# Attention mask as 64 rows of the score stacks, one stack per head, in place of mask matmuls and GpSimd selects

## What is computed

```python
x = x + 0.5 * ffn(layernorm(x))    # 8 experts, each token to its best one, hidden width 512
x = x + attn(layernorm(x))
x = x + 0.5 * ffn(layernorm(x))

def attn(x):
    xn = x * rsqrt(mean(x * x) + EPS) * norm_w
    q, k, v = heads(xn @ Wq.T + bq), heads(xn @ Wk.T + bk), heads(xn @ Wv.T + bv)   # 16 heads of 8
    scores = einsum('bhqd,bhkd->bhqk', q, k) / sqrt(8)
    scores = where(triu(ones((256, 256)), k=1), -inf, scores)
    out = einsum('bhqk,bhkd->bhqd', softmax(scores), v)
    return xn + out @ Wo.T + bo
```

## Time and profile before

| | |
|---|---|
| median of three runs | 322.96 us |
| profiled execution, its span | 319.3 us |
| PE busy | 276.5 us (87%) |
| DVE busy | 214.5 us (67%) |
| POOL busy | 178.8 us (56%) |
| ACT busy | 159.7 us (50%) |
| attention loop | about 127 to 240 us of the span |
| expert parts | about 41 to 86 and 264 to 308 us |

### The profile page before, as it was taken

The page is one execution under the profiler, slowest core; times in us unless marked ns, Lnnn a source line. Parts: engine busy times, 40 slices in busy tenths (PEclk is TensorE's granted clock), DMA queues, the critical chain, the costliest instruction groups (busy, mean ns, idle before and its releaser), DMA issues.

```text
span 319.3 us, 7990 instructions
## 1 busy us (share of the span) xinstructions
PE 276.5 (87%) x2396; PEld 224.1 (70%) x2396; DVE 214.5 (67%) x691; ACT 159.7 (50%) x389; POOL 178.8 (56%) x319
## 2 busy tenths in 40 slices
PE   8573999999995776999999999998977699999960
PEld 8463999999994363656666566665646588999960
DVE  3877048788608759987666777776787555888850
ACT  2430076666204834586666667768541107666620
POOL 5577815554525201587777787788657730554551
PEclk9855999999999998799999999999976579999996
DMA  6973141220040731662524522110001143222100
GB/s 180 403 293 119 53 95 54 65 63 31 24 126 8 199 121 53 197 180 88 156 79 134 152 72 74 57 53 6 3 19 42 42 121 86 51 67 71 34 10 0
DMA packets 34387, 29.37 MB, mean 92 GB/s; under 512 B 4108, under 2 KB 28817, under 8 KB 34352
## 3 DMA queue, kind: packets, MB, share of 16 engines
q1 hardware_dynamic: 29696, 23.52, 24.6%
q0 software_dynamic: 2496, 4.27, 4.1%
q10 hardware_dynamic: 2160, 1.14, 1.4%
HBM read 17.08 MB, written 12.55 MB: 93 GB/s over the span
## 4 chain that ended last, share of the span: by engine, by line
PE 58%; POOL 11%; DVE 10%; issue 7%; DMA 5%; ACT 4%; POOLq 1%; ACTq 0%; SPq 0%; DVEq 0%
PE bank L1279 13%; PE bank L1290 12%; PE bank L1207 5%; PE bank L1436 3%; PE bank L1408 3%; PE bank L1384 3%; POOL pT L541 2%; POOL row L454 2%; PE bank L1381 2%; PE bank L1414 2%; PE bank L1271 2%; POOL disp_d L462 2%; PE bank L1240 2%; PE bank L1466 2%; PE bank L1389 1%
## 5 line engine op out<-in xcount | busy, mean ns | idle before, releaser
L723 ACT ACTIVATE pT<-bank 128x512 f32<-128x512 f32 x96 | 56.4, 599 | 36.2 <-PE bank L1414 25.2
L1207 PE MATMUL bank<-zero 128*128 128x128 f32 x298 | 43.2, 314 | 9.4 <-DVE rowi L916 4.7
L1279 PE MATMUL bank<-xsT,ew 128*128 128x128 f32 x368 | 48.8, 276 | 0.2
L1290 PE MATMUL bank<-experts,hT 128*128 x368 | 48.9, 276 | 0.0
L1207 PEld LDWEIGHTS bank<-zero 128*128 128x128 f32 x298 | 41.6, 227 | 10.1 <-DVE rowi L916 4.7
L1038 DVE TENSOR_REDUCE mh<-bank 128x2 f32<-128x512 f32 x64 | 42.1, 682 | 8.5 <-PE bank L1384 8.2
L541 POOL TENSOR_SCALAR_AFFINE_SELECT pT<-pT 128x512 f32<-128x512 f32 x62 | 39.8, 643 | 10.2 <-ACT pT L723 9.9
L1279 PEld LDWEIGHTS bank<-xsT,ew 128*128 128x128 f32 x368 | 44.7, 192 | 0.7 <-ACT xsT L621 0.3
L1290 PEld LDWEIGHTS bank<-experts,hT 128*128 128x128 f32 x368 | 44.8, 192 | 0.5 <-issue 0.3
L627 ACT ACTIVATE hT<-bank,ew 128x128 f32<-128x128 f32 x92 | 28.8, 364 | 28.9 <-PE bank L1279 28.9
L923 DVE TENSOR_SCALAR hT<-bank,ew 128x128 f32<-128x128 f32 x92 | 28.0, 346 | 20.2 <-PE bank L1279 18.9
(11 more groups left out here) (133 smaller groups left out, 479.4 us busy)
## 6 DMA issues: line engine op xcount, KB each, us to landing
sp_d<-spl SPq DMA_DIRECT2D x32, 192.0 KB, 2.6
experts<-in_experts SPq DMA_DIRECT2D x8, 578.0 KB
qz<-sp_d SPq DMA_DIRECT2D x32, 96.0 KB
ks<-sp_d SPq DMA_DIRECT2D x32, 96.0 KB
xs_sb<-disp_d SPq DMA_DIRECT2D x46, 66.0 KB, 1.8
row<-in_x SPq DMA_DIRECT2D x4, 256.0 KB, 5.5
row<-x_d SPq DMA_DIRECT2D x4, 256.0 KB, 5.0
disp_d<-pad ACTq DMA_DIRECT2D x12, 66.0 KB, 2.3
```

The lines of the kernel that those rows point to most:

```text
L723: act.activation(pT[:, u, :], bank[2 + u % 2][:, :], ACT.Exp, scale=SCALE).then_inc(a_e, 1)
L1207: pe.matmul(bank[b][:, 0:P], zero[:, :], zero[:, :], start=True, stop=True)
L1279: mm = pe.matmul(bank[2 + 2 * (k % 2) + c // 2][:, (c % 2) * P:(c % 2 + 1) * P], ew[:, k % WRING, c * P:(c + 1) * P], xsT[:, k % 2, :], st ...
L1290: mm = pe.matmul(bank[6 + k % 2][:, 0:D], hT[:, k % 2, c, :], w2.rearrange("p a c -> p (a c)"), start=(c == 0), stop=(c == HC - 1))
```

## The change

The contraction grows to 128 rows and carries the mask itself. A stack now holds one head: rows 0 to 47 the parts, 48 to 50 the maxima (-1 on the side of `ks`), 63 to 127 the mask: one row for each of the 64 blocks of two tokens (for the last block one in each half of the sequence, so 65), whose products of powers of two give a sum of at most -2^45 where a key is later than its query, and exactly zero elsewhere. `ks` has as many stacks as `qz`, 16 each. Every unit of either product becomes four matmuls of 128 columns, one a head, with weights of its own. Blocks that need no mask use 65 rows. The identity matmuls, the selects, DVE's `last_mask`, the table `low` and the semaphore `a_pm` are gone; `pv` waits for the exponentials themselves.

The constant rows come from a new input, `tri` (128 x 512 float32, 256 KB), loaded by the sync engine ahead of the expert weights. `stack_fill` is now a broadcast copy of it: POOL fills one `qz`, ACT the other `qz` and both `ks`, between the exponentials of the first routing and behind the pad rows. Since the queries' product now passes the rows of the maxima, `stack_load` for sequences from 2 on first writes zeros over them with a DMA of its own, and the waits of `scores_q` count 80 instead of 64 for these.

```diff
-JROWS = BLK * HD
-SROWS = 2 * JROWS
+SROWS = BLK * HD
 MROW = SROWS
 KROWS = MROW + 3
+TROW = 65
+UP, DOWN, NEXT, FAR = 40, -41, 5, 86
...
+def stack_rows():
+    c = np.zeros((P, 2, T), np.float32)
+    c[MROW:KROWS, 1, :] = -1
+    t = np.arange(T)
+    for row, block, half in ([(TROW - 2, P // 2 - 1, 0), (TROW - 1, P // 2 - 1, 1)]
+                             + [(TROW + r, r, None) for r in range(P // 2 - 1)]):
+        here = np.ones(T, bool) if half is None else t // P == half
+        n = t % P
+        last = block == P // 2 - 1
+        c[row, 0, here & (n == 2 * block)] = 2.0 ** UP
+        if not last:
+            c[row, 0, here & (n == 2 * block + 1)] = 2.0 ** DOWN
+        c[row, 1, here & (n == 2 * block + 1)] = -2.0 ** NEXT
+        c[row, 1, here & (n > 2 * block + 1)] = -2.0 ** FAR
+    return c.reshape(P, 2 * T)
...
-        ks = [sb(f"ks{i}", [P, NPAIR, T], BF16) for i in range(2)]
+        ks = [sb(f"ks{i}", [P, 2, 2, 4, T], BF16) for i in range(2)]
+        tri = sb("tri", [P, 2 * T])
...
+            sp.dma_start(tri[:, :], tri_in).then_inc(tri_s, 16)
...
                 need(sp, a_st, 12 * (b - 2) + 6 * half + 6)
+                if not isinstance(b, int) or b >= 2:
+                    sp.dma_start(qz[k][MROW:KROWS, half, :, :, :].rearrange("s j i n -> s (j i) n"),
+                                 zero[MROW:KROWS, :].bitcast(BF16).unsqueeze(1).broadcast_to((3, 8, T))
+                                 ).then_inc(a_stk[k][half], 16)
                 for j in range(2):
-                    rows_j = slice(JROWS * j, JROWS * (j + 1))
-                    for t, buf in ((0, qz[k][rows_j, half, j, :, :]),
-                                   (1, ks[k][rows_j, 4 * half:4 * half + 4, :])):
+                    for t, buf in ((0, qz[k][0:SROWS, half, j, :, :]),
+                                   (1, ks[k][0:SROWS, half, j, :, :])):
...
-                pool.memset(qz[k][:, :, :, :, :].rearrange("p h j i n -> p (h j i n)").bitcast(F32), 0.0
-                            ).then_inc(static_s, 1)
-                pool.memset(ks[k][:, :, :].rearrange("p g n -> p (g n)").bitcast(I32), NEG1_PAIR
-                            ).then_inc(static_s, 1)
+                pool.wait_ge(tri_s, 16)
+                pool.tensor_copy(qz[k][:, :, :, :, :].rearrange("p h j i n -> p (h j i) n"),
+                                 tri[:, 0:T].unsqueeze(1).broadcast_to((P, NH, T))).then_inc(static_s, 1)
...
             route_exp(0, 1)
+            stack_fill(qz[0], 0)
             route_exp(0, 2)
+            stack_fill(ks[0], 1)
             pad_rows(0, range(NE))
+            stack_fill(ks[1], 1)
...
-            last_mask(2)
             add_out(6)
-            last_mask(3)
...
             def scores_q(b, bh, k, half, u):
-                    pe.wait_ge(a_stk[k][half], 64 * (bh + 1))
+                    pe.wait_ge(a_stk[k][half], 80 * bh + 64)
...
+                ov = o[:, :].rearrange("p (h n) -> p h n", h=4)
+                for h in range(4):
+                    if w < 2:
+                        i, j, late, kt, rows_ = 2 * pp + w, h // 2, 1, h % 2, P if h % 2 else TROW
+                    else:
+                        i, j, late, kt, rows_ = 2 * pp + h // 2, h % 2, 0, 0, P
+                    mm = pe.matmul(ov[:, h, :], qz[k][0:rows_, half, j, i, late * P:(late + 1) * P],
+                                   ks[k][0:rows_, half, j, i, kt * P:(kt + 1) * P],
+                                   start=True, stop=True, **MM_BANK)
...
-                pe.wait_ge(a_pm, 8 * b + 4 * half + 2 * pp + 2)
+                pe.wait_ge(a_e, 12 * b + 6 * half + 3 * pp + 3)
```

More of the change, by code:

```diff
@@ L527, in max_split @@
                 pool.tensor_tensor(s_[:, :, 2, :], r_, z_, ALU.add).then_inc(a_mb, 1)
-            def mask(b, half, pp, late):
-                pool.wait_ge(a_e, 12 * b + 6 * half + 3 * pp + 2 + late)
-                n = 2 * pp + late
-                need(pool, a_pm, 8 * b + 4 * half + n - 3)
-                if not isinstance(b, int):
-                    pool.tensor_tensor(turn[:, n:n + 1], zero[:, 0:1], zero[:, 0:1], ALU.add)
-                if late:
-                    p_ = pT[:, 3 * pp + 2, :].rearrange("p (h n) -> p h n", h=4)
-                else:
-                    p_ = pT[:, 3 * pp:3 * pp + 2, :].rearrange("p u (j n) -> p (u j) n", j=2)[:, :, 0:P]
-                pool.affine_select(out=p_, in_=p_, pattern=[[0, 4], [1, P]], compare_op=ALU.is_ge, fill=0.0,
-                                   base=0, channel_multiplier=-1).then_inc(a_pm, 1)
             def step(b, half, more=True):
@@ L548, in step @@
                     max_split(b + 1, 0)
-                for n in range(4 if more or half == 0 else 2):
-                    mask(b, half, n // 2, n % 2)
+                for n in range(4):
                     if isinstance(b, int) and b >= 6:
@@ L1404, in scores_k @@
                 o = bank[2 + u % 2]
-                if w < 2:
-                    pair = 4 * half + 2 * pp + w
-                    ov = o[:, :].rearrange("p (j n) -> p j n", j=2)
-                    mm = pe.matmul(ov, ks[k][0:KROWS, pair, 0:P], qz[k][0:KROWS, half, :, pair - 4 * half, :],
-                                   start=True, stop=True, **MM_BANK)
-                else:
-                    ov = o[:, :].rearrange("p (i j n) -> p i j n", i=2, j=2)
-                    for i in range(2):
-                        pair = 4 * half + 2 * pp + i
-                        mm = pe.matmul(ov[:, i, :, :], ks[k][0:KROWS, pair, P:T],
-                                       qz[k][0:KROWS, half, :, pair - 4 * half, P:T],
-                                       start=True, stop=True, **MM_BANK)
+                ov = o[:, :].rearrange("p (h n) -> p h n", h=4)
+                for h in range(4):
+                    if w < 2:
+                        i, j, late, qt, rows_ = 2 * pp + w, h // 2, 0, h % 2, TROW if h % 2 else P
+                    else:
+                        i, j, late, qt, rows_ = 2 * pp + h // 2, h % 2, 1, 1, P
+                    mm = pe.matmul(ov[:, h, :], ks[k][0:rows_, half, j, i, late * P:(late + 1) * P],
+                                   qz[k][0:rows_, half, j, i, qt * P:(qt + 1) * P],
+                                   start=True, stop=True, **MM_BANK)
                 mm.then_inc(a_st, 1)
             def pv(b, k, half, pp):
-                pe.wait_ge(a_pm, 8 * b + 4 * half + 2 * pp + 2)
+                pe.wait_ge(a_e, 12 * b + 6 * half + 3 * pp + 3)
                 if pp == 0:
```

68 lines of the change are left out of this document (17 added, 51 removed).

## The result

| | kernel before | changed kernel |
|---|---|---|
| median of 11 runs each, side by side | 322.88 us (320.8 to 324.1) | 319.79 us (317.8 to 321.6) |
| ratio, 95% interval | | 0.9914 (0.9888 to 0.9940) |
| profiled execution, its span | 319.3 us | 317.8 us |
| starts of sequences 1 and 7 | 141.24, 221.93 | 143.26, 221.72 |

The change brings 3.1 us, where 7.6 were predicted. The time lies within the range; the size of the gain was wrong by more than half.

A forecast was written before the change was run, and what follows sets the result against it. The prediction took PE to set the pace by a small margin, with stack loads directly behind and deciding after the change. Terms -1.9, -1.5, -1.6, -1.8 and -0.8 sum to -7.6 us: 315.4 us, range 308.5 to 322.

The forecast's parts named there:

- PE's pace: Attention loop: each unit becomes eight pairs at 55 ns, 0.44 us, saving 1.76 us a sequence; PE alone would allow 11.5.
- rival C: PE in the loop: pairs run slower than 55 ns, 0.65 us a unit, about 326 us in all; chance 0.04.
- Rival D: Loop: with fewer PE columns the granted clock falls to 1.2 GHz, each 7 us at half costing some 3; chance 0.03.
- The load: Sync engine's queue: with the zeros ahead, a half's stack load lands 6.6 us after first issue, in place of 5.8.
- Rival B: Stack loads, all into partitions 0 to 47, land later; no gain at 7.9 us, 327 at 2 us more; chance slower 0.08.
- the prediction's own sign: Loop: a period above 13.4 us with PE waiting for DMA at starts of halves would mean Rival B.
- the wait that sets the period: Loop: the load's landing sets periods of 12.8 (sequences 1 to 3, -1.9 us) and 12.5 (4 and 5, -1.5).
- POOL's selects at zero in the loop: Attention loop: removing POOL's 62 selects of 643 ns counts for nothing beyond what PE gets.
- Rival A: Loop: the loads don't bind and PE does, six sequences at 11.5 us each, 308.7 us; chance 0.15.
- Opening and sequence 0: Before sequence 1: PE's saved columns give -1.8 us, half of the bounds 0 and -3.5.
- The last sequence: Last sequence and routing: without DVE's two masks, POOL's 0.84 us idle ahead of a scale goes; -0.8 us, up to -2.
- The front: Before the loop: ACT's three fills, at most 4.8 us each, and POOL's fill cost 0, up to 2 us if uncovered.

The follow-up runs named there:

- e1: The changed kernel without the DMA of zeros ahead of each stack load, old maxima left in their rows; 311.91 us, ratio 0.9701.
- e14: e11 with POOL's 62 selects and DVE's two masks put back; 320.36 us, ratio 0.994 to the kernel before.
- e7: The changed kernel with POOL's 62 selects and DVE's two masks put back; 322.54 us, ratio 0.999.
- e11: The changed kernel with only the order of channels changed, so a stack's 48 rows lie at one distance in DRAM; 310.67 us, ratio 0.963.
- e13: The kernel before with the channel order of e11 and nothing else changed; 321.96 us, ratio 0.997.
- e0: The kernel before run once more, unchanged; 322.93 us, ratio 1.0017.
- e4: The changed kernel with the zeros inside the load as a seventh block, in place of a DMA of their own; 314.25 us, ratio 0.974.
- e12: e4 with two DMAs a load in place of four and the channel order of e11; 310.89 us, ratio 0.966.
- e6: The changed kernel with the DMA of zeros cut to one row of 512 bytes, old maxima left in their rows; 318.27 us, ratio 0.985.

## Why the prediction was wrong, point by point

- **PE's pace** was right. 58 ns a pair measured, 55 taken; rival C (81 ns) is out. Rival D is out as well: the granted clock is 1.00 from 132.5 us on to the end of the loop in the changed kernel.
- **The load** was right in size: 6.6 us from first issue to landing predicted, 6.9 measured, 6.0 before. Rival B is out in the form that it had: partitions 0 to 47 for all four DMAs cost nothing (e1: 5.8). The swizzle (the Trainium skill, DMA: Bandwidth & Descriptors, section The descriptor swizzle), which the prediction weighed beside it, is for a transfer over 128 partitions. What counted is the shape of the transfer, and by its 7 increments the load was on few engines before the change too. By the prediction's own sign (a period above 13.4 with waits for DMA) sequences 4 and 5 would read as B; their landing of 6.9, short of B's 7.9, says that they aren't.
- **The step that failed is the wait that sets the period.** The prediction took it from the load's landing and added 0.4 us a sequence for the maxima in sequences 4 and 5, none in 1 to 3, though the earlier trace rows showed 3.34 us for their landing. In the changed kernel the maxima are issued 3.9 us after the load begins (more where stores stand between), land last, and cost PE 7.9 us of waiting from 140 to 220. The terms: sequences 1 to 3 -1.1 (predicted -1.9), 4 and 5 +0.6 (predicted -1.5), 6, with no load of its own, -1.7 (predicted -1.6): in the loop 2.8 us short of the forecast. The medians are 4.5 short; the rest lies in the opening and sequence 0, by the points below, and isn't priced apart. In the kernel before the same transfer stands behind four DMAs, lands in 2.2 to 3.3 and has room: the one issued at 185.23 serves a half that starts at 188.36.
- **POOL's selects at zero in the loop**, a gain put down to PE, was the second failed reading. Busy shares of 15.3 of 20 looked like room; but POOL's work lies in a ring with ACT's exponentials and PE, and e14 gives it 9.7 us at PE's pace. The sum wasn't spoilt by it, since the change takes out selects and mask matmuls together; that was luck. Of the mask matmuls alone the same reading would have expected the gain in the loop, and e7 shows 0.4 us.
- **Rival A** (PE binds, 308.7) is what the change is worth once the loads are out of the way: e11 has 310.7. Its arithmetic gave 11.5 us a period; 12.0 is the mean of six in e11 ((212.19 - 140.46) / 6).
- **Opening and sequence 0** was predicted at -1.8 and is +2.0 in the two profiles, outside its bounds. With equal stretches of half clock the start of sequence 1 is at 143.46 (e13) against 143.26 (changed kernel) with 13.6 us of them, and at 141.24 and 142.31 (before, e0) against 139.74 and 140.00 (e4, e12) with 6.8. So it is -0.2 to about -1.9 (e4 and e12 differ from the changed kernel in their loads too), and the granted clock of the two profiles hid it.
- **The last sequence** gave -1.3 (97.35 to 96.07 us from its start to the end), predicted -0.8. The idle time of the earlier trace rows is gone. Part of it can be the clock: the first profile has 20.5 us at half clock between 234 and 259, this one 17.1, and e0, with 17.1 as well, takes 96.94, which makes it -0.9.
- **The front** cost nothing, as predicted: the fills take 3.6 us each, and ACT's first tile of the first expert part is read at 40.25 (before 39.93).
- **Around the span** lie 1.8 us and not 3.7: the profiled execution of the changed kernel took 319.61 at a span of 317.8. The profiled execution of the kernel before was one of its faster ones.
- **The mask's sum** is not exactly zero for every key that may be seen, as the section on the change has it: a query at an odd place meets its own key in one row, 2^-41 times -2^5, and gets -2^-36, except at the last place of each 128.

## What to carry over

When a change shortens the engine that is busy all the time, list every ring that closes in the same period, and price each at the new pace: an engine with idle time, or a transfer that lands half a microsecond early, can be as near as the one that shows. For a small transfer on the path, ask when the large one beside it has drained; the shape of a DMA on its DRAM side (six blocks, or 48 equal steps) decided more here than its place in a queue, its issuer or its number of issues. The two kernels with the mask rows and the new order of channels (e11 and e12) are the fastest of all, equal within the noise, and compute the whole block: 310.7 and 310.9 us against 323.0.

## What the hardware showed unexpectedly

- A 12 KB transfer of three partitions takes 2.2 us alone, 2.2 to 4.6 while a 384 KB load is in flight whose DMAs show 7 increments, and 2.1 to 2.9 when they show 16. Where it took 2.5 or more beside a load of 7, it mostly landed 0.2 to 0.3 us after the load.
- The same 192 packets of 2 KB, 84 ns each in the median, are at most 8 or 9 at a time with the source in six blocks and 14 to 19 with 48 equal steps.
- The issue of a 96 KB DMA took 0.70 to 0.77 us with the source in six blocks and mostly 0.42 with 48 equal steps; a DMA of 512 bytes took 0.59 (e6), stores of 192 KB mostly 0.37 to 0.53.
- The same small transfer issued from ACT's own queue, some 0.4 us sooner after the start of the sync engine's load, took 3.4 us to land against 2.9 and so gained nothing; its issue (0.73 us) held up ACT's next exponential.
